# One transposition and one correction product per pair of tiles in a fused convolution, mixing and adapter kernel

## The chip, the cores and the metric

The kernel runs on 1 core of one Trainium2 chip. The metric is the device time of one execution in microseconds (us), and less is better. PE is the matrix engine, DVE the vector engine, ACT the scalar engine, POOL the general engine, SP the engine that here only issues transfers. "Ln" is line n of the kernel before.

## The reference

The input x has 128 samples of 64 channels by 1024 steps. Four residual layers follow each other. Layer 0 is a long convolution by channel, masked by length; layer 1 mixes the channels with one of 16 matrices; layers 2 and 3 are dense over the 1024 steps with low-rank adapters, chosen by one id of 32 (rank 16) and one label of 5 (rank 32).

```python
def _L2_cond_ref(x, adapter_ids, base_weight, base_bias, lora_A_w, lora_B_w):
    result = jnp.einsum('bsd,od->bso', x, base_weight) + base_bias
    A = lora_A_w[adapter_ids]
    Bw = lora_B_w[adapter_ids]
    h = jnp.einsum('bsd,brd->bsr', x, A)
    lora_out = jnp.einsum('bsr,bor->bso', h, Bw)
    return result + lora_out

def _L3_cond_ref(x, labeler_index, W, lora_A, lora_B_w):
    base = jnp.einsum('bsi,oi->bso', x, W)
    labelers_A = lora_A[labeler_index]
    low = jnp.einsum('bsi,bir->bsr', x, labelers_A)
    delta = jnp.einsum('bsr,or->bso', low, lora_B_w) * LORA_SCALING
    return base + delta

x = x + _L0_cond_ref(x, itok_B_8_3872, ...)
x = x + _L1_cond_ref(x, itok_B_0_15, ...)
x = x + _L2_cond_ref(x, itok_B_6_15, ...)
x = x + _L3_cond_ref(x, itok_B_0_2, ...)
```

## The kernel before

The work has three stages. In the **setup** (to about 177 us) PE multiplies the two dense layers, each with the identity added for the residual, into one 1024 by 1024 matrix. It also makes what the adapters need: `b2_0` to `b2_3` (the B factors of layer 2 carried through layer 3), `c` (how the layer-2 B factors meet the layer-3 A factors), the bias carried through layer 3 as one row (`row`, from `b3t`), and the bias against the layer-3 A factors (`c_row`). The setup is a list of jobs, `ORDER`; each has one of four areas of PSUM (the accumulators) and waits until the area's last user is read out. In the **convolution** (to about 545 us) PE runs one channel after the other. The **dense stage** (to the end) is the one that the change is about.

The dense stage takes the 128 samples as 64 tiles of two samples (128 rows: 2 by 64 channels), and two tiles (`v` = 0 and 1) make a pair `n`, so there are 32 pairs. Every engine has one written-out order per pair (`pair(n, last_one)` in `dense_tensor`, `dense_vector`, `dense_scalar`, `dense_sync`, `dense_gpsimd`) and runs it in order. Pairs 1 to 30 (to 29 on SP) are a hardware loop. Engines meet only at semaphores, and a wait holds everything behind it on its engine.

The two tiles are cut into halves `a11`, `a21`, `a22`, `a12` and multiplied with seven products in place of eight, after Strassen: M1, M5, M2, M4 (`wide_product`, L782: 24 instructions each, whose right half also carries 96 adapter columns) and M6, M3, M7 (`plain_product`, L792: 12 instructions each). Values are split into a high and a low part, in three passes. M1 and M2 share the accumulator S, M5 and M4 V, M6 and M7 P, M3 uses Q.

For the adapters of tile `v` the order is: DVE copies the low-rank values h out of PSUM to `hrow` (`h_rows`, L677); PE transposes them (`turn`, L772); DVE copies them to `hc` (`h_columns`, L685); PE multiplies with `c_gath` (`adapters`, L777), which adds to the layer-3 values what the layer-2 adapter and the bias put into them; DVE splits the result into `hs` (`h_stack`, L689); PE multiplies `hs` with the gathered B factors `stack` (`low_rank`, L800), once for the left and once for the right half of the outputs. `low_rank(0, 0)` ends by raising `lr11_done`. SP loads the rows of `stack` (`load_stack`, L434) and of `c_gath` (`load_c`, L475), after it has read ids into registers (`ids`, L409).

While PE works on pair `n`, it also mixes the channels for pair `n + 1` in four pieces, `quarter(n + 1, 0)` to `quarter(n + 1, 3)` (L759). All four write the same accumulator bank, `MIX_BANK`. ACT reads each piece out (`take`, L564) and raises `quarter_read`; the next piece waits for it:

```python
            if bank == MIX_BANK:
                ready(pe, quarter_read, 4 * n + q)
```

ACT's order in the middle of a pair stands at L598 to L609:

```python
            if not last_one:
                take(n + 1, 0, a11, xa11)
            act.wait_ge(lr11_done, n + 1)
            act.wait_ge(pair_sums, 2 * n + 2)
            copy(halves(y_out[0][:, 0:HB]), of_s, ACT.Copy).then_inc(y11_copied, 1)
            ...
            if not last_one:
                take(n + 1, 1, a21)
                h_high(act, n + 1, 0)
                h_high(act, n + 1, 1)
```

`h_high` (L442, its activations are L449) writes the high parts of the adapters' A factors of pair `n + 1` into the weights, and `h_low` (L458, L465) on DVE the low parts. After `h_low` DVE makes sums of the mixed pieces (`sums`, L669: L671, L672, L675), and then adds M7 to the output (L745), which raises `u3_read`; PE's last piece of a pair, `low_rank(1, HB)`, waits for it.

Of the kernel before, what the change touches and what calls it, by code (L numbers as in the profile page):

```python
# [12 lines left out]
P = 128  # L13
# [10 lines left out]
KC = 2 * R2 + 2  # L24
# [17 lines left out]
def program(nc, x, xt_in, steps, cond, adapter, labeler, log_dt, ssm_c, log_a_real, a_imag, ssm_d,  # L42
# [64 lines left out]
    ones, o = at("ones", [P, 1], F32, o)  # L107
# [27 lines left out]
    c_row, o = at("c_row", [1, LR], F32, o)  # L135
    assert o <= o_w[2]
# [82 lines left out]
    hc = both("hc", [P, P])  # L219
    hs = both("hs", [P, 2, P], F32R)  # L220
    c_gath = both("c_gath", [P, P])
    late = place("late", [P, HB], U16)
    assert o == o_last
    o += 8 * T
# [5 lines left out]
    hrow = both("hrow", [P, P])  # L230
# [10 lines left out]
    c_d = nc.dram_tensor("c_d", [AR + 1, LR], F32).ap()  # L241
    b3_d = nc.dram_tensor("b3_d", [R3, 2, T], F32).ap()
    row_d = nc.dram_tensor("row_d", [2, T], F32).ap()
# [51 lines left out]
    split_const, const_stored, b3_scaled = sem("split_const"), sem("const_stored"), sem("b3_scaled")  # L295
    bias_ready = sem("bias_ready")
# [66 lines left out]
    c_adapters = c_d[0:AR].rearrange("(a r) c -> a r c", r=R2)  # L363
# [49 lines left out]

    def load_tables(eng, v, a, l):
# [17 lines left out]
    masked = sem("masked")  # L432

    def load_stack(eng, v, a):  # L434

        for b in range(2):
            row = b * (R2 + R3)
            eng.dma_start(f(stack[v][row:row + R2]), b2_d[bass.ds(a[b], 1)].squeeze(0)).then_inc(stack_landed[v], 16)
            eng.dma_start(f(stack[v][KS + row:KS + row + R2, 0]),
                          b2_d[bass.ds(a[b], 1), :, 0, :].squeeze(0)).then_inc(stack_landed[v], 16)  # L440
# [27 lines left out]
    def dense_sync(sp):  # L468
# [6 lines left out]
        def load_c(v, a, l):  # L475
            for b in range(2):
                rows = slice(b * (R2 + R3), b * (R2 + R3) + R2)
                cols = bass.ds(l[b] * R3, R3)
                sp.dma_start(c_gath[v][rows, H3], c_adapters[bass.ds(a[b], 1), :, cols].squeeze(0)).then_inc(c_landed[v], 16)
                sp.dma_start(c_gath[v][KS + b:KS + b + 1, H3], c_d[AR:AR + 1, cols]).then_inc(c_landed[v], 16)  # L480
# [3 lines left out]
        for v in range(2):  # L484
            for to, of in ((stack[v][H3], b3_d), (stack[v][KS + R2:KS + R2 + R3, 0], b3_d[:, 0]), (stack[v][KS:KS + 2, 1], row_d)):
# [5 lines left out]
        sp.wait_ge(c_fixed, 2)  # L491
# [5 lines left out]
        def stacks(n):  # L497

            if isinstance(n, int) and n == 0:
                for v in range(2):  # L500
                    load_stack(sp, v, first_ids[v])
                return
            sp.wait_ge(p_done, n)
            for v in range(2):
                load_stack(sp, v, ids(sp, n, v, B))

        def pair(n, last_one):
# [7 lines left out]
            a, l = [ids(sp, n + 1, v, B) for v in range(2)], [ids(sp, n + 1, v, 2 * B) for v in range(2)]  # L515
# [3 lines left out]
            sp.wait_ge(adapted, 2 * n + 2)  # L519
# [9 lines left out]
    def dense_gpsimd(pool):  # L529
        pool.wait_ge(x1_stored[1], stored_all)  # L530
        for v in range(2):
            pool.wait_ge(x1_landed[v], LANDED_FIRST)
        for v in range(2):
            nc.gpsimd.tensor_copy(c_gath[v][:], ident[:]).then_inc(gfixed, 1)
        pool.wait_ge(gfixed, 4)
        for v in range(2):
            nc.gpsimd.memset(c_gath[v][:, KS:P], 0.0).then_inc(c_fixed, 1)
        pool.wait_ge(c_fixed, 2)
        fixed = [0]

        def fix(ins):
            fixed[0] += 1
            ins.then_inc(small_fixed, 1)
            pool.wait_ge(small_fixed, fixed[0])

        for v in range(2):
            fix(nc.gpsimd.memset(hrow[v][:], 0.0))
            fix(nc.gpsimd.memset(hc[v][:], 0.0))
# [1228 lines left out]
```

## Time and profile before

| | us |
|---|---|
| median of 3 runs | 1446.25 |
| lowest and highest run | 1444.93, 1446.51 |
| the profiled execution, its own time | 1442.18 |
| its span, first to last instruction | 1440.4 |
| PE busy in it | 1429.8 (99%) |
| DVE busy | 1127.4 (78%) |
| ACT busy | 612.7 (43%) |
| POOL busy | 100.9 (7%) |

The times of instructions are from the one profiled execution, counted from the start of its span. A matrix instruction's start is when it enters the engine, and the next one enters before it ends, so what a group costs PE is the distance between starts. When its result can be read is told by its end.

### The profile page before, as it was taken

The page shows a single profiled execution, that of the slowest core. Times are in us where ns is not written, and L with a number is a line of the kernel's source. Part 1 is how long each engine was busy: PE and PEld are TensorE (multiplying, and loading weights), DVE is VectorE, ACT ScalarE, POOL GpSimd, SP SyncE. Part 2 cuts the span into 40 slices and gives each one's busy share as a digit, 9 for nine tenths or more (in the row PEclk, how much of TensorE's full clock was granted, in tenths as well). Part 3 has the DMA queues.
Part 4 walks back from the last instruction along what each step waited for, and adds up shares of the span by engine and source line. Part 5 has one row for each costly group of instructions (what it writes and reads, how often), then busy time and mean ns, then how long its engine had stood idle before and what let it go on. Part 6 is the DMA issues. An engine that isn't in the chain of part 4 may idle for free.

```text
span 1440.4 us, 31629 instructions
## 1 busy us (share of the span) xinstructions
PE 1429.8 (99%) x9368; PEld 1329.8 (92%) x9368; DVE 1127.4 (78%) x2288; ACT 612.7 (43%) x1217; POOL 100.9 (7%) x193
## 2 busy tenths in 40 slices
PE   9999999999999999999999999999999999999998
PEld 7888899999999999999999999999999999999997
DVE  7975498888888887777777777787777777778775
ACT  4331376666666663333433433433343343343331
POOL 2322100000000002000000000000000000000000
PEclk9999999999999999999999999999999999999999
DMA  8033288888888886564564565556556556555652
GB/s 315 1 129 79 76 283 272 276 277 272 277 268 276 273 274 183 170 203 148 166 200 146 162 197 163 153 182 190 153 162 204 146 161 203 153 153 190 182 154 81
DMA packets 117070, 271.94 MB, mean 189 GB/s; under 512 B 24173, under 2 KB 60401, under 8 KB 114381
## 3 DMA queue, kind: packets, MB, share of 16 engines
q1 hardware_dynamic: 107048, 237.86, 54.1%
q10 hardware_dynamic: 9990, 33.68, 5.8%
q8 instruction: 17, 0.28, 0.1%
q14 instruction: 15, 0.12, 0.0%
HBM read 198.59 MB, written 72.85 MB: 188 GB/s over the span
## 4 chain that ended last, share of the span: by engine, by line
PE 95%; DVE 2%; DMA 2%; SPq 0%; issue 0%; POOL 0%; ACT 0%; DVEq 0%; POOLq 0%; ACTq 0%
PE ps L796 18%; PE ps L789 17%; PE ps L1704 14%; PE ps L788 12%; PE ps L769 8%; PE ps L1603 7%; PE ps L1715 6%; PE ps L805 4%; PE ps L1695 3%; PE ps L1707 2%; PE ps L1589 1%; PE ps L780 1%; PE ps L1612 1%; DMA p<-in_L_cond_base_weight 1%; DMA out<-y_out 1%; PE ps L775 1%
## 5 line engine op out<-in xcount | busy, mean ns | idle before, releaser
L789 PE MATMUL ps<-weights,xa 128*128 128x352 f32 x1152 | 323.0, 322 | 0.0
L788 PE MATMUL ps<-weights,xa 128*128 128x256 f32 x1152 | 321.8, 281 | 0.5 <-ACT y_out L597 0.5
L796 PE MATMUL ps<-weights,xs 128*128 128x512 f32 x1152 | 291.2, 401 | 0.0
L796 PEld LDWEIGHTS ps<-weights,xs 128*128 128x128 f32 x1152 | 207.0, 189 | 40.4
L1704 PE MATMUL ps<-toep,ut 128*128 128x512 f32 (+2 forms) x1152 | 226.7, 342 | 0.0
L788 PEld LDWEIGHTS ps<-weights,xa 128*128 128x128 f32 x1152 | 217.3, 189 | 2.5 <-issue 1.1
L789 PEld LDWEIGHTS ps<-weights,xa 128*128 128x128 f32 x1152 | 216.2, 188 | 1.3
L1704 PEld LDWEIGHTS ps<-toep,ut 128*128 128x128 f32 x1152 | 194.3, 189 | 16.6
L568 ACT ACTIVATE a<-ps 128x512 f32<-128x512 f32 x128 | 76.7, 599 | 281.9 <-PE ps L769 281.2
L769 PE MATMUL ps<-m_gath,x_in 128*128 128x128 f32 x1024 | 134.6, 275 | 1.3 <-DVE x_in L660 1.3
L769 PEld LDWEIGHTS ps<-m_gath,x_in 128*128 128x128 f32 x1024 | 126.6, 191 | 4.0 <-DVE x_in L660 1.5
L1196 ACT ACTIVATE ut<-xt 128x896 fp32r<-128x896 f32 x64 | 61.2, 956 | 138.4 <-PE ps L1715 131.0
L651 DVE COPY_PREDICATED x_in<-late,x_nat 128x512 f32<-128x512 uint16 x124 | 92.8, 748 | 18.9 <-DVE late L646 18.7
L1715 PE MATMUL ps<-toep,ut 128*128 128x256 f32 x768 | 107.3, 289 | 0.0
L789 PE MATMUL ps<-weights,xs 128*128 128x352 f32 x384 | 106.6, 320 | 0.0
L788 PE MATMUL ps<-weights,xs 128*128 128x256 f32 x384 | 105.2, 278 | 0.0
L382 POOL COPY m_gath<-mix 64x64 f32 x128 | 49.5, 387 | 788.8 <-PE ps L769 689.2
L1603 PE MATMUL ps<-p,staged 128*128 128x512 f32 x432 | 99.1, 390 | 0.0
L1603 PEld LDWEIGHTS ps<-p,staged 128*128 128x128 f32 x432 | 80.8, 188 | 18.0 <-DVE c_row L1474 0.9
L1715 PEld LDWEIGHTS ps<-toep,ut 128*128 128x128 f32 x768 | 95.8, 190 | 0.0
L1523 DVE TENSOR_TENSOR ut<-xt,ut 128x896 fp32r<-128x896 f32 x64 | 69.9, 1092 | 16.2 <-ACT ut L1196 16.2
L449 ACT ACTIVATE weights<-tab 128x128 fp32r<-128x128 f32 (+1 forms) x256 | 71.5, 354 | 23.1 <-DVE tab L456 23.1
(227 smaller groups left out, 2255.3 us busy)
## 6 DMA issues: line engine op xcount, KB each, us to landing
xt<-in_xt SPq DMA_DIRECT2D x64, 512.0 KB, 5.7
x_d<-yo SPq DMA_DIRECT2D x64, 512.0 KB, 2.9
x_nat<-in_x SPq DMA_DIRECT2D x64, 512.0 KB, 3.8
lags<-kern_d SPq DMA_DIRECT2D x63, 512.0 KB, 5.0
x_in<-x_d SPq DMA_DIRECT2D x62, 512.0 KB
out<-y_out ACTq DMA_DIRECT2D x62, 512.0 KB, 5.8
stack<-b_d SPq DMA_DIRECT2D x130, 128.0 KB, 3.9
tab<-a_d SPq DMA_DIRECT2D x128, 128.0 KB, 2.1
```

The source lines that it names most:

```text
L449: ins = nc.scalar.activation(to, of, ACT.Copy)
L568: ins = copy(raw[:], mixing, ACT.Copy)
L651: nc.vector.copy_predicated(x1_in[v][:, cols], late[:], x_nat[v][:, cols]).then_inc(chosen[v], 1)
L769: ins = mm(acc[:, bank, i * P:(i + 1) * P], x1_in[v][:, c * P:(c + 1) * P], m_gath[v][:], start=True, stop=True)
L788: mm(acc[:, left, 0:HALF], x_part, w[:, 0:HALF], start=start, stop=end, skip_group_check=True)
L789: ins = mm(acc[:, right, 0:HALF + KR], x_part, w[:, HALF:WIDE], start=start, stop=end, skip_group_check=True)
L796: ins = mm(acc[:, bank], operand[:, a, i, :], plain(i, b, m), start=opens and i == a == b == 0, stop=i == K4 - 1 and a == 1, skip_group_ch ...
L1196: copy(ut[u % 2][:, 0, 0:SPLIT], xt[u % BUFS][:, 0:SPLIT], ACT.Copy).then_inc(ut_hi, 1)
L1523: tt(ut[u % 2][:, 1, 0:SPLIT], xt[u % BUFS][:, 0:SPLIT], f(ut[u % 2][:, 0, 0:SPLIT]), ALU.subtract).then_inc(ut_lo, 1)
L1603: ins = mm(t[:, cols], staged[n % 2][:, a, c, :], p3[:, c, b, cols], start=c == a == b == 0, stop=c == K8 - 1 and a == 1)
L1704: mm(y[:, half * HB + i * P:(half + 1) * HB], xs[:, a, half * half_t + i, :], tp[:, b, 0:HB - i * P], start=i == a == b == 0, stop=False)
L1715: ins = mm(y[:, to:to + QT], xs[:, a, i, :], tp[:, b, at_col:at_col + QT], start=False, stop=i == half_t - 1 and a == 1)
```

## The change

The dense stage now handles both tiles of a pair together in `turn` and `adapters`:

- `hrow`, `hc` and `c_gath` exist once, with tile 0 in rows or columns 0 to 63 and tile 1 in 64 to 127. `turn(n)` transposes both tiles at once, between the halves of M6; the one inside M4 is gone. `adapters(n)` is one product, after `quarter(n + 1, 1)`.
- `low_rank(0, 0)` and its `lr11_done` come behind M3 instead of behind M6, directly ahead of `quarter(n + 1, 2)`.
- On DVE one `h_columns(n)` comes after `first_low(n + 1)`, and both `h_stack` come after the addition of M6 (L738).
- The bias no longer passes through `c_gath`. The setup makes one bias row per label (`row_d` has 5 rows of two parts), for which `c_row` is made earlier, behind the job `a3b`, turned by five small products into `crt`, and multiplied with `b3n`. The job `row` so has four products of 512 columns (each two instructions) in place of two, and waits for `b3_scaled` and `crt_ready`. SP loads the chosen labels' rows into `stack` in every pair: 12 transfers of `stack` and 4 of `c_gath` per pair, before 8 and 8.
- Tile 1 has its high and low parts in the other order of rows, so that DVE reads and writes its 64 rows where they lie.
- SP reads four ids with one load (`pair_ids`).
- ACT's order in the dense stage is as it was.

```diff
+    HIGH, LOW = (0, KS), (KS, 0)
+    def load_stack(eng, v, a, l):
...
+            high, low, bias = HIGH[v] + row, LOW[v] + row, LOW[v] + 2 * b
+            eng.dma_start(f(stack[v][high:high + R2]), b2_d[bass.ds(a[b], 1)].squeeze(0)).then_inc(stack_landed[v], 16)
+            eng.dma_start(f(stack[v][low:low + R2, 0]), b2_d[bass.ds(a[b], 1), :, 0, :].squeeze(0)).then_inc(stack_landed[v], 16)
+            eng.dma_start(f(stack[v][bias:bias + 2, 1]), row_d[bass.ds(l[b], 1)].squeeze(0)).then_inc(stack_landed[v], 16)
...
             h_rows(n, 0)
-            h_columns(n, 0)
             if not last_one:
                 choose(n + 1, 1, 0)
             dve.wait_ge(m4_done, n + 1)
             h_rows(n, 1)
-            h_stack(n, 0)
-            h_columns(n, 1)
             if not last_one:
                 first_low(n + 1)
+            h_columns(n)
+            if not last_one:
                 choose(n + 1, 1, 1)
-            h_stack(n, 1)
             dve.wait_ge(m6_done, n + 1)
             dve.wait_ge(pair_sums, 2 * n + 2)
             tt(y_out[0][:, HB:T], y_out[1][:, HB:T], of_p, ALU.add).then_inc(u2_read, 1)
+            for v in range(2):
+                h_stack(n, v)
...
-            wide_product(xa22, M4, V_LEFT, V_RIGHT, FRONT, False)
-            turn(n, 0)
-            wide_product(xa22, M4, V_LEFT, V_RIGHT, BACK, False).then_inc(m4_done, 1)
-            adapters(n, 0)
+            wide_product(xa22, M4, V_LEFT, V_RIGHT, ALL, False).then_inc(m4_done, 1)
             if not last_one:
                 quarter(n + 1, 0)
             pe.wait_ge(s2_lo, n + 1)
             ready(pe, y22_added, n)
             plain_product(xs2, M6, P_BANK, FRONT, True)
-            turn(n, 1)
+            turn(n)
             plain_product(xs2, M6, P_BANK, BACK, False).then_inc(m6_done, 1)
-            pe.wait_ge(hs_lo, 2 * n + 1)
-            pe.wait_ge(stack_landed[0], 64 * n + 64)
-            if isinstance(n, int) and n == 0:
-                pe.wait_ge(rows_landed, 16 * 6)
-            low_rank(0, 0, PIECES_S).then_inc(lr11_done, 1)
-            adapters(n, 1)
             if not last_one:
                 quarter(n + 1, 1)
+            adapters(n)
             pe.wait_ge(s4_lo, n + 1)
             ready(pe, y12_added, n)
             plain_product(xs4, M3, Q_BANK, ALL, True)
+            pe.wait_ge(hs_lo, 2 * n + 1)
+            pe.wait_ge(stack_landed[0], 96 * n + 96)
+            if isinstance(n, int) and n == 0:
+                pe.wait_ge(rows_landed, 16 * 4)
+                pe.wait_ge(stack_cleared, 1)
+            low_rank(0, 0, PIECES_S).then_inc(lr11_done, 1)
             if not last_one:
                 quarter(n + 1, 2)
...
-            over_chunks(t[0:1, HB + LR:HB + 2 * LR], lambda c: bias_col[:, c:c + 1], lambda c: a3raw[:, c, :]).then_inc(job_done, 1)
+            for l in range(L3N):
+                ins = mm(t[0:R3, HB + LR + l:HB + LR + l + 1], c_row[:, l * R3:(l + 1) * R3], ones[0:1, 0:1], start=True, stop=True)
+            ins.then_inc(job_done, 1)
             t = job("row")
             pe.wait_ge(bias_ready, 1)
+            pe.wait_ge(b3_scaled, 1)
             for half in range(2):
                 cols = slice(half * HB, (half + 1) * HB)
-                ins = mm(t[0:1, cols], ones[:], b3t[:, cols], start=True, stop=True)
+                mm(t[0:L3N, cols], ones[:], b3t[:, cols], start=True, stop=False)
+            pe.wait_ge(crt_ready, 1)
+            for half in range(2):
+                cols = slice(half * HB, (half + 1) * HB)
+                ins = mm(t[0:L3N, cols], crt[B3_ROWS], b3n[B3_ROWS, cols], start=False, stop=True)
```

How the instructions move is shown for the loop over the pairs. First PE before, from M6 to M7 (`xs2` to `xs3`; `m_gath` with `x1_in` is a quarter, `stack0` with `hs0` is `low_rank(0, ...)`):

```order
L796 MATMUL ps<-weights_49,xs2_158 128x512 x6
L805 MATMUL ps<-stack0_171,hs0_178 128x256 [waits stack_landed0,hs_lo]
L805 MATMUL ps<-stack0_171,hs0_178 128x256 x3
L780 MATMUL ps<-hc1_177,c_gath1_181 128x128 [waits hc_ready,c_landed1]
...
L769 MATMUL ps<-m_gath1_187,x1_in1_175 128x128 [waits quarter_read]
L769 MATMUL ps<-m_gath1_187,x1_in1_175 128x128 x3
L796 MATMUL ps<-weights_49,xs4_159 128x512 [waits y12_added,x_s4_lo]
L796 MATMUL ps<-weights_49,xs4_159 128x512 x11
...
L769 MATMUL ps<-m_gath1_187,x1_in1_175 128x128 [waits quarter_read]
```

The same stretch of PE in the change:

```order
L804 MATMUL ps<-weights_49,xs2_160 128x512 x6
...
L775 MATMUL ps<-m_gath1_187,x1_in1_177 128x128 [waits quarter_read]
L775 MATMUL ps<-m_gath1_187,x1_in1_177 128x128 x3
...
L788 MATMUL ps<-hc_178,c_gath_181 128x128 [waits hc_ready,hs_lo,c_landed1,c_landed0]
L804 MATMUL ps<-weights_49,xs4_161 128x512 [waits y12_added,x_s4_lo]
L804 MATMUL ps<-weights_49,xs4_161 128x512 x11
...
L813 MATMUL ps<-stack0_173,hs0_179 128x256 [waits stack_landed0]
L813 MATMUL ps<-stack0_173,hs0_179 128x256 x3
...
L775 MATMUL ps<-m_gath1_187,x1_in1_177 128x128 [waits quarter_read]
```

The first `low_rank` stood ahead of the second quarter; now it stands behind M3, directly ahead of the third quarter (the last row of both pieces). The correction product (`hc` with `c_gath`) has moved behind the second quarter.

ACT in the change, from its reading of the first quarter to that of the third; the same instructions stood in the same order before:

```order
L572 ACTIVATE a11_166<-ps 128x512 [waits mixed]
L574 ACTIVATE xa11_156<-ps 128x512
L605 ISA [waits lr11_done]
L606 ACTIVATE y_out0_171<-ps 128x512 [waits pair_sums]
...
L572 ACTIVATE a21_167<-ps 128x512 [waits mixed]
...
L461 ACTIVATE weights_49<-tab2_0_190 128x4x2x16 [waits tab_landed0]
...
L461 ACTIVATE weights_49<-tab2_1_184 128x4x2x16 [waits diffed]
...
L572 ACTIVATE a22_168<-ps 128x512 [waits mixed]
```

Nothing moved on ACT: its wait for `lr11_done` stands ahead of its reading of the second quarter (`a21`) in both.

## Rows read from the trace of the kernel before

**Rows 1.** The page: PE's busy time, and the granted clock in 40 slices
```profile
PE 1429.8 (99%) x9368; PEld 1329.8 (92%) x9368; DVE 1127.4 (78%) x2288; ACT 612.7 (43%) x1217; POOL 100.9 (7%) x193
...
PEclk9999999999999999999999999999999999999999
```

**Rows 2.** Waits of PE, whole span: us in total, times, longest
```profile
PE ps L769 <- DVE x_in L660: 1.3, 1, 1.3
PE ps L788 <- ACT y_out L597: 0.5, 1, 0.5
```

**Rows 3.** Timeline of PE, 814 to 831 us: start, length, engine, line, what, count
```profile
816.25 0.38 PE L780 MATMUL ps<-hc,c_gath 128*128 128x128 f32 x2
816.46 1.06 PE L769 MATMUL ps<-m_gath,x_in 128*128 128x128 f32 x8
817.28 1.63 PE L796 MATMUL ps<-weights,xs 128*128 128x512 f32 x6
...
820.24 0.64 PE L805 MATMUL ps<-stack,hs 128*128 128x256 f32 x4
820.72 0.39 PE L780 MATMUL ps<-hc,c_gath 128*128 128x128 f32 x2
820.95 1.06 PE L769 MATMUL ps<-m_gath,x_in 128*128 128x128 f32 x8
821.76 3.00 PE L796 MATMUL ps<-weights,xs 128*128 128x512 f32 x12
824.60 1.05 PE L769 MATMUL ps<-m_gath,x_in 128*128 128x128 f32 x8
...
829.97 0.72 PE L805 MATMUL ps<-stack,hs 128*128 128x512 f32 x2
830.52 0.29 PE L788 MATMUL ps<-weights,xa 128*128 128x256 f32 x1
830.64 0.32 PE L789 MATMUL ps<-weights,xa 128*128 128x352 f32 x1
```

**Rows 4.** Timeline of ACT, same pair
```profile
821.00 0.60 ACT L602 ACTIVATE y_out<-ps 128x512 f32<-128x512 f32 x1 [2.36 <-PE ps L805]
822.04 0.60 ACT L568 ACTIVATE a<-ps 128x512 f32<-128x512 f32 x1 [0.44 <-PE ps L769]
822.53 1.11 ACT L449 ACTIVATE weights<-tab 128x128 fp32r<-128x128 f32 x4
```

**Rows 5.** Timeline of DVE, same pair
```profile
816.44 0.42 DVE L682 COPY hrow<-ps 64x48 f32<-64x48 f32 x2
...
819.26 0.67 DVE L667 TENSOR_TENSOR xa<-a,xa 128x512 fp32r<-128x512 f32 x1
...
821.14 0.42 DVE L692 CAST hs<-ps 64x256 fp32r<-64x256 f32 x1
...
826.80 0.69 DVE L671 TENSOR_TENSOR s<-a,a 128x512 f32<-128x512 f32 x1 [0.42 <-ACT xa L570]
...
828.80 0.68 DVE L745 TENSOR_TENSOR y_out<-y_out,ps 128x512 f32<-128x512 f32 x1
```

**Rows 6.** Timeline near 591 us, the dense stage's one wait of PE
```profile
590.61 0.60 ACT L597 ACTIVATE y_out<-ps 128x512 f32<-128x512 f32 x1 [2.99 <-DMA out<-y_out]
...
591.36 0.36 PE L788 MATMUL ps<-weights,xa 128*128 128x256 f32 x1 [0.52 <-ACT y_out L597]
...
591.55 0.32 PE L789 MATMUL ps<-weights,xa 128*128 128x352 f32 x1
```

**Rows 7.** Timeline at 1403 us, a pair whose adapter tables had landed early
```profile
1402.95 2.13 ACT L449 ACTIVATE weights<-tab 128x128 fp32r<-128x128 f32 x8
...
1404.10 2.24 DVE L465 TENSOR_TENSOR weights<-tab,weights 128x128 fp32r<-128x128 f32 x8 [0.54 <-ACT weights L449]
```

**Rows 8.** Timeline of the setup, PE and DVE
```profile
105.24 1.88 PE L1670 MATMUL ps<-b3t,ones 128*1 128x512 f32 x4
...
129.03 4.24 PE L1679 MATMUL ps<-fac_v,fac_u 128*32 128x32 f32 x128
...
104.03 1.23 DVE L1416 TENSOR_TENSOR b_out<-ps,b_out 128x1024 fp32r<-128x1024 f32 x1 [4.96 <-ACT b_out L1134]
...
110.09 0.68 DVE L1478 TENSOR_SCALAR b3t<-b3t 32x1024 f32<-32x1024 f32 x1 [1.73 <-DMA b3t<-in_L_cond_lora_B_w]
```

More of the change, by code:

```diff
@@ L23 @@
 KS = 2 * R2 + R3
-KC = 2 * R2 + 2
 ROUND = 1.5 * 2.0 ** 23
@@ L135, in program @@
     c_row, o = at("c_row", [1, LR], F32, o)
+    b3n, _ = at("b3n", [P, T], F32, o_c - AR // P * 4 * T)
     assert o <= o_w[2]
@@ L229, in program @@
     m_gath = both("m_gath", [P, P])
-    hrow = both("hrow", [P, P])
+    hrow = place("hrow", [P, P])
     x_nat[1], o = at("x_nat1", [P, T], F32, o_rest + 4 * T + 4 * TFOLD)
@@ L476, in load_c @@
             for b in range(2):
[L477 to L480, printed above, removed]
+                row = v * KS + b * (R2 + R3)
+                to = c_gath[row:row + R2, v * KS + R2:v * KS + R2 + R3]
+                sp.dma_start(to, c_adapters[bass.ds(a[b], 1), :, bass.ds(l[b] * R3, R3)].squeeze(0)).then_inc(c_landed[v], 16)
         sp.dma_start(x1_d[:, C - 1], yo[(C - 1) % 2][:]).then_inc(x1_stored[1], 16)
@@ L484, in dense_sync @@
         for v in range(2):
-            for to, of in ((stack[v][H3], b3_d), (stack[v][KS + R2:KS + R2 + R3, 0], b3_d[:, 0]), (stack[v][KS:KS + 2, 1], row_d)):
+            high, low = HIGH[v] + R2, LOW[v] + R2
+            for to, of in ((stack[v][high:high + R3], b3_d), (stack[v][low:low + R3, 0], b3_d[:, 0])):
                 sp.dma_start(f(to), of).then_inc(rows_landed, 16)
@@ L514, in pair @@
             stacks(n)
-            a, l = [ids(sp, n + 1, v, B) for v in range(2)], [ids(sp, n + 1, v, 2 * B) for v in range(2)]
+            a, l = pair_ids(n + 1, B), pair_ids(n + 1, 2 * B)
             for v in range(2):
@@ L770, in quarter, with turn, adapters @@
             ins.then_inc(mixed, 1)
-        def turn(n, v):
-            pe.wait_ge(hrow_ready, 2 * n + v + 1)
-            ready(pe, hs_lo, 2 * n + v)
-            nc.tensor.transpose(acc[:, SMALL_BANK, 0:P], hrow[v][:], ident[:]).then_inc(turned, 1)
-        def adapters(n, v):
-            pe.wait_ge(c_landed[v], 64 * n + 64)
-            pe.wait_ge(hc_ready, 2 * n + v + 1)
-            mm(acc[:, SMALL_BANK, P:2 * P], c_gath[v][:], hc[v][:], start=True, stop=True).then_inc(adapted, 1)
+        def turn(n):
+            pe.wait_ge(hrow_ready, 2 * n + 2)
+            ready(pe, hc_ready, n)
+            nc.tensor.transpose(acc[:, SMALL_BANK, 0:P], hrow[:], ident[:]).then_inc(turned, 1)
+        def adapters(n):
+            for v in range(2):
+                pe.wait_ge(c_landed[v], 32 * n + 32)
+            pe.wait_ge(hc_ready, n + 1)
+            ready(pe, hs_lo, 2 * n)
+            mm(acc[:, SMALL_BANK, P:2 * P], c_gath[:], hc[:], start=True, stop=True).then_inc(adapted, 1)
         def wide_product(operand, m, left, right, chunks, opens):
@@ L800, in low_rank @@
         def low_rank(v, col, pieces):
-            for j, rows in ((0, P), (1, KS + 2)):
+            for j, rows in ((0, P), (1, (KS + 4, P)[v])):
                 at_col = col
@@ L894, in _ @@
             sp.dma_start(a3_d.rearrange("l p n -> p l n"), lora3_out[:].rearrange("p l c r -> p l (c r)")).then_inc(a3_stored, 16)
+            sp.dma_start(b3n[B3_ROWS], lora3_b).then_inc(in_b3, 16)
             for m in range(4):
```

131 lines of the change are left out of this document (66 added, 65 removed).

## The prediction, on record before the changed kernel ran

> **What bounds the kernel now.** I read the engines' busy times first: PE is busy for 1429.8 of 1440.4 us at the full granted clock, and no other engine is near it [rows 1]. Then PE's waits: in the 32 pairs of the dense stage it waits once, for 0.5 us [rows 2]. So what PE no longer does is a gain, and any new wait of PE is a loss, one for one. Last I read the timelines of one pair, since the change moves work past waits, and a busy total can't tell how late each of them is [rows 3 to 5].
>
> **What PE saves.** One transposition: M6 with one inside takes 2.96 us from start to start (817.28 to 820.24), M3 with the same 12 products takes 2.84 (821.76 to 824.60) [rows 3]. That is 0.12 us, and I take it for the one inside M4. One correction product: 0.21 us (816.25 to 816.46) or 0.23 (820.72 to 820.95) [rows 3], so 0.22. Together 0.34 us per pair, 10.9 us in 32 pairs.
> The Trainium skill ("TensorE: Matmul & The Clock Gate", Part 4: PE-mode transpose) gives a 128 by 128 transposition about 275 ns in one kernel's context. By that 32 of them would save 8.8 us and not 3.8, and the sum would come out 5 us lower. The row has the transposition overlapped by its neighbours, so I keep 0.12.
>
> **What is moved without cost.** Count from the end of M4, 816.25. DVE has `hrow` copied at +0.6 [rows 5]; `turn` now comes at +2.3 (a quarter of 0.82, half of M6). Its result is there near +2.6; DVE is then in `first_low`, which was over at +3.7 [rows 5] and now starts 0.2 earlier, so `hc` is ready near +3.8. `adapters` comes at 0.82 + 2.96 + 0.81 = +4.6: 0.8 us to spare. DVE then has two mask steps and one copy under mask (about 1.3 us), the addition of M6 (0.7) and the two `h_stack` (L692 with 0.42 [rows 5] and a subtraction, about 0.7 each). The first is ready near +6, and `low_rank(0, 0)` comes at 4.6 + 0.22 + 2.84 = +7.7. Nothing waits there. On SP, 12 plus 4 transfers stand for 8 plus 8, and four loads of ids for twelve, so the adapter tables come no later by more than the 2 us of four `stack` issues; the chain below reads them over 2 us later than today. POOL's preparation is about as long as it was. I cost these at nothing; if SP came much later, `h_high` would wait and everything below grow with it.
>
> **The new wait, first part.** `low_rank(0, 0)` raises `lr11_done`. ACT stands at that wait before it reads the second quarter, and the third quarter may not start until that reading is done, since they share a bank. Before, the product came ahead of the second quarter, and ACT had its copy L602 behind it while PE did the second quarter and M3. Now the product is the last thing ahead of the third quarter. Let S be its start. ACT's copy starts at S + 0.76 (820.24 to 821.00 [rows 3, 4]). The reading L568 can follow 0.49 later (the distance of ACT's next two starts, 822.04 to 822.53) and takes 0.60 [rows 4]: done at S + 1.85. PE restarts 0.15 after such an end (591.21 to 591.36 [rows 6]): S + 2.00. Without the wait it would be S + 0.48 (820.24 to 820.72 [rows 3]). So PE stands for 1.52 us. The pipe's refill costs 0.07: the product after the restart is 0.19 behind (591.36 to 591.55), else 0.12 (830.52 to 830.64) [rows 6, 3].
>
> **Second part.** Behind that reading ACT writes the adapters' high parts for both tiles, now 3.6 us later against M6 than before. They start at S + 1.25 + 0.49 = S + 1.74. DVE's low parts start 1.15 behind and take 2.24 where nothing else holds them [rows 7]: S + 5.13. Then come the sums and L745, whose start is 2.00 behind the first sum's (826.80 to 828.80) and which takes 0.68 [rows 5]: S + 7.81, and with 0.15 PE may start its last piece, which waits for `u3_read`, at S + 7.96. PE itself is there at S + 2.07 + 5.37 = S + 7.44 (third quarter to last piece, 824.60 to 829.97 [rows 3]). So it waits 0.52 and refills for 0.07.
>
> **The setup.** The job `row` gets two more products, 4 instructions of 0.47 each: 1.88 us; 10 instructions of one column at the price of the smallest shown, 4.24 / 128 = 0.033 each: 0.33 us [rows 8]. It also waits for `b3_scaled`. DVE ends the last `b2` part at 105.26, then scales for 0.68 [rows 8]; a copy of one row moved ahead of it adds some 0.3: 106.2, with 0.15 for the restart 106.4. PE is there at 105.24 + 0.33 = 105.6. So 0.8 of wait, 3.0 us in all, all of it on PE's path. Bounds: 2.2 without that wait, 4 if the transfer of `b3n` or the small products are later.
>
> **The sum.** Per pair 1.52 + 0.07 + 0.52 + 0.07 - 0.34 = +1.84 us. The waits exist only where a next pair is mixed, in 31 pairs: +57.0. The last pair saves 0.34. With the setup: 57.0 - 0.3 + 3.0 = +59.7 us. Against the profiled execution's own 1442.18 that gives 1501.9. That execution lies 4.1 us below the median of the runs, 1446.25; the same difference on the median gives **1506 us**.
>
> **Rivals.**
> (a) Only the first wait is there: DVE or ACT run a little tighter than the rows laid end to end, and the last piece finds `u3_read` up. For it: 0.52 us is a small difference of two long chains. Against it: each distance in the chain is one that the trace shows without a wait in it. Then 1.52 + 0.07 - 0.34 = 1.25 per pair, +38.8 - 0.3 + 3.0: 1488.
> (b) A third wait. M2 and M4 wait for ACT's copies L592 and L597, which wait for the stores of the pair before; PE has already lost 0.5 us there once [rows 2, 6]. The output is finished later against the next M1 than today, and more `stack` transfers start sooner beside the stores. At that row's price, 0.5 us in each of 31 pairs, +15.5: 1522.
> (c) It gets faster. The third quarter's wait costs nothing, because the reading of the second quarter is over by then. That holds if ACT reads the quarter ahead of its wait for `lr11_done`, or if that product comes 1.5 us or more ahead of the third quarter. Then only the saving and the setup are left: -10.9 + 3.0, 1438. The order on ACT and PE in the change speaks against both: the product stands directly ahead of the quarter, and ACT's wait ahead of the reading.
> (d) The waits let the granted clock fall. PE has waited 1.3 us ahead of the dense stage with no slice below full [rows 1, 2], and the new waits are 1.5 us and shorter, with longer stretches of products between them. I give it no case of its own.
>
> **How the numbers follow.** The forecast with both waits has 0.72, (a) 0.12, (b) 0.12, (c) 0.03, and 0.01 is left for no change. The range from 1486 to 1524 takes in (a) and (b) with the bounds of the setup. Within 0.2% (3 us), which is about what a measurement of this kernel can tell from no change, I give 0.01; faster 0.03; slower 0.96.
>
> **What would show it.** PE's waits should have a row for L775 (the quarters) behind ACT's reading L572, 31 times, about 1.5 us each, and one for L813 (`low_rank`) behind DVE L751, 31 times, about 0.5 us. PE's busy time should fall by about 8 us (10.9 saved, 2.2 added) while the span grows by 60. ACT's wait for PE ahead of L606 should grow, since the product comes 3 us later against M6. A distance from pair to pair that has not grown, or waits of PE behind SP's transfers or behind L596 and L601, would make the prediction wrong. If the change is slower but these two rows are not there, the reason is wrong too.

## The result, and the profile after

| | before | changed |
|---|---|---|
| median of 6 runs | 1445.29 us (1443.25 to 1446.51) | 1534.06 us (1530.36 to 1538.81) |
| span of the profiled execution | 1440.4 us | 1532.1 us |
| ratio, 95% interval | | 1.0617 [1.0595, 1.0638] |

The change makes the kernel 6.2% slower. I had forecast slower, and 1506 us; the time lies 28 us above that and outside my range of 1486 to 1524.

The page of the changed kernel, the lines that answer to [rows 1]:

```profile
PE 1451.6 (95%) x9286; PEld 1327.1 (87%) x9286; DVE 1118.6 (73%) x2256; ACT 601.7 (39%) x1217; POOL 96.4 (6%) x187
...
PEclk9999999999999999999999999999999999999999
```

The granted clock is full in every slice (mean 1.000), so the loss is not TensorE's clock: PE stands. Its waits, and two of ACT's (us in total, times, longest), which answer to [rows 2]:

```profile
ACT y_out L606 <- PE ps L813: 205.7, 32, 12.5
...
ACT y_out L596 <- DMA out<-y_out: 97.1, 30, 4.2
...
PE ps L775 <- ACT a L572: 39.0, 31, 1.3
...
PE ps L796 <- ACT y_out L596: 22.5, 29, 1.8
...
PE ps L813 <- DVE y_out L751: 8.2, 31, 0.3
...
PE ps L1682 <- DVE b3n L1479: 2.3, 1, 2.3
```

The two waits that I had forecast are there, 31 times each. The row between them is one that I had only as a rival: PE's M2 (L796) waits for ACT's copy L596 of M1's result, and that copy waits for a store.

One pair of the changed kernel, the timeline of all engines cut to the chain (start, length, engine, line, what, count):

```profile
880.56 0.39 PE L788 MATMUL ps<-hc,c_gath 128*128 128x128 f32 x2
...
880.70 3.02 PE L804 MATMUL ps<-weights,xs 128*128 128x512 f32 x12
...
883.56 0.63 PE L813 MATMUL ps<-stack,hs 128*128 128x256 f32 x4
884.31 0.60 ACT L606 ACTIVATE y_out<-ps 128x512 f32<-128x512 f32 x1 [6.23 <-PE ps L813]
884.80 0.59 ACT L572 ACTIVATE a<-ps 128x512 f32<-128x512 f32 x1
885.28 2.13 ACT L461 ACTIVATE weights<-tab 128x128 fp32r<-128x128 f32 x8
...
885.45 1.16 PE L775 MATMUL ps<-m_gath,x_in 128*128 128x128 f32 x8 [1.26 <-ACT a L572]
...
886.36 2.98 PE L804 MATMUL ps<-weights,xs 128*128 128x512 f32 x12
886.43 2.24 DVE L477 TENSOR_TENSOR weights<-tab,weights 128x128 fp32r<-128x128 f32 x8 [3.26 <-ACT weights L461]
...
890.12 1.05 PE L775 MATMUL ps<-m_gath,x_in 128*128 128x128 f32 x8
890.70 0.69 DVE L751 TENSOR_TENSOR y_out<-y_out,ps 128x512 f32<-128x512 f32 x1
...
891.36 0.86 SPq L482 DMA_DIRECT2D x_in<-x_d  x2
...
891.44 0.74 PE L813 MATMUL ps<-stack,hs 128*128 128x512 f32 x2 [0.27 <-DVE y_out L751]
...
892.01 0.35 PE L796 MATMUL ps<-weights,xa 128*128 128x256 f32 x1
...
892.14 0.34 ACTq L623 DMA_DIRECT2D out<-y_out  x1
...
898.84 0.60 ACT L596 ACTIVATE y_out<-ps 128x512 f32<-128x512 f32 x1 [3.18 <-DMA out<-y_out]
...
899.58 0.36 PE L796 MATMUL ps<-weights,xa 128*128 128x256 f32 x1 [0.62 <-ACT y_out L596]
```

Read it from S = 883.56, the start of the moved product. ACT copies at S + 0.75, reads the second quarter until S + 1.83, and PE goes on at S + 1.89; I had S + 2.00. DVE's L751 starts at S + 7.14 and PE's last piece at S + 7.88; I had S + 7.96. Then comes the wait that my sum had at nothing. SP issues the two loads of x1 at 891.36, since they wait only for the last quarter. The store, on ACT's queue, waits for DVE's sums, which are late, and goes out at 892.14, 0.78 us behind the first load. It lands when ACT's copy starts, at 898.84. In the kernel before, the first load went out 0.03 us ahead of the store, and the second 0.50 us behind it.

Where a pair's time went, from first product to first product in the trace, where nothing else is said (means over the 32 pairs, in the last two columns over the 31 that have a next one; us). M1, M5, M2 and M4 follow each other in this order, and a product here is two instructions, of which the first counts:

| | M1 to M5 | M5 to M2 | M2 to M4 | M4, first to last product | M4's last to the next M1 | pair |
|---|---|---|---|---|---|---|
| before | 3.30 | 3.29 | 3.34 | 3.20 | 14.56 | 27.68 |
| changed | 3.39 | 4.18 | 3.44 | 3.08 | 16.39 | 30.52 |

The pairs take 31 x 2.84 = 88.1 us more, the setup 4.9. The last pair, from its M1 to the end of the span, takes 1.3 less (28.16 for 29.46). The span grew by 91.7.

### The profile page after: what moved, and what is told of

Read it like the earlier page. It is cut to its first block, busy times and chain, and to the rows that moved or that the text cites. A ratio compares the mean times of both kernels' runs of the same rounds, so it can differ in the third digit from the quotient of the medians.

```text
span 1532.1 us, 31101 instructions
## 1 busy us (share of the span) xinstructions
PE 1451.6 (95%) x9286; PEld 1327.1 (87%) x9286; DVE 1118.6 (73%) x2256; ACT 601.7 (39%) x1217; POOL 96.4 (6%) x187
## 4 chain that ended last, share of the span: by engine, by line
PE 73%; DMA 14%; DVE 4%; issue 4%; ACT 4%; SPq 0%; POOL 0%; ACTq 0%; DVEq 0%; POOLq 0%
PE ps L804 17%; PE ps L1720 13%; DMA out<-y_out 13%; PE ps L797 9%; PE ps L775 8%; PE ps L796 7%; PE ps L1731 6%; PE ps L1610 4%; PE ps L1711 3%; PE ps L813 3%; PE ps L1723 2%; ACT a L572 1%; ACT y_out L596 1%; PE ps L1619 1%; ACT xa L574 1%
## 5 line engine op out<-in xcount | busy, mean ns | idle before, releaser
L796 PE MATMUL ps<-weights,xa 128*128 128x256 f32 x1152 | 326.1, 284 | 22.7 <-ACT y_out L596 22.5
L796 PEld LDWEIGHTS ps<-weights,xa 128*128 128x128 f32 x1152 | 217.2, 189 | 36.5 <-issue 36.3
L477 DVE TENSOR_TENSOR weights<-tab,weights 128x128 fp32r<-128x128 f32 (+1 forms) x256 | 71.8, 354 | 101.0 <-ACT weights L461 101.0
L796 PE MATMUL ps<-weights,xs 128*128 128x256 f32 x384 | 106.3, 280 | 0.0
L606 ACT ACTIVATE y_out<-ps 128x512 f32<-128x512 f32 x32 | 19.1, 597 | 205.7 <-PE ps L813 205.7
```

The lines of the kernel that those rows point to most:

```text
L477: ins = nc.vector.tensor_tensor(to, of, f(high), ALU.subtract)
L796: mm(acc[:, left, 0:HALF], x_part, w[:, 0:HALF], start=start, stop=end, skip_group_check=True)
```

## The experiments

Ratios are to the kernel before, run in turn with each kernel on the same chip. "Head start" is the time from the issue of the first x1 load to that of the first tile's store; "landing" is the time from the store's issue to the start of ACT's copy that waits for it. Both are medians over 26 pairs.

**1. ACT's order exchanged** (changed kernel; e1_act_order)

```diff
+            if not last_one:
+                take(n + 1, 1, a21)
+                h_high(act, n + 1, 0)
+                h_high(act, n + 1, 1)
             act.wait_ge(lr11_done, n + 1)
...
             if not last_one:
-                take(n + 1, 1, a21)
-                h_high(act, n + 1, 0)
-                h_high(act, n + 1, 1)
                 act.wait_ge(a22_lo, n + 1)
```

> The change, with ACT reading the second quarter and writing both tiles' high parts ahead of its wait for lr11_done. Theory (the order on ACT behind that wait makes PE's waits at the third quarter and at the last low_rank): both rows of PE, 39.0 and 8.2 us of waiting in the change, go to 0. The third wait (M2 behind ACT's copy of M1, 22.5 us) follows from the order in which transfers start: if it comes from the stack transfers starting sooner against the store, it falls below 8 us, since without the two waits the store starts 0.2 us sooner against M1 and the stack transfers 0.5 us later; the time is then 1436 to 1446 us. Rival A (the third wait has its own cause in the change, whatever the two others do): it stays above 18 us and the time is about 1465. Rival B (the two waits come from the single correction product or from DVE's order, not from ACT's): the rows stay, 1520 or more.

Measured: 1437.57 us (1437.02 to 1438.77), ratio 0.9947 [0.9931, 0.9964]. PE's waits:

```profile
PE ps L1683 <- DVE b3n L1480: 2.4, 1, 2.4
...
PE ps L797 <- ACT y_out L596: 0.8, 1, 0.8
...
PE ps L814 <- DVE y_out L752: 0.4, 1, 0.4
```

Of the three rows of the pairs the first has gone, and the two others are left with one time each. A pair takes 27.32 us against 27.64 (medians): 0.32 saved, and I had forecast 0.34. So everything that the change loses in the pairs comes from ACT's order against the moved product. With it put right, the change is a gain.

**2. Only the reading of the second quarter ahead of the wait; the adapters' high parts stay behind it**

```diff
+            if not last_one:
+                take(n + 1, 1, a21)
             act.wait_ge(lr11_done, n + 1)
...
-                take(n + 1, 1, a21)
                 h_high(act, n + 1, 0)
```

> The change, with only the reading of the second quarter ahead of ACT's wait for lr11_done; the high parts stay behind it. Theory (two chains from the same product): the wait at the third quarter goes (39.0 us to 0), but PE's wait at the last low_rank behind DVE grows from 8.2 us to about 45 (1.5 us in each of 31 pairs), since that chain gets only 0.5 us shorter while PE comes 1.4 us sooner. Per pair 0.5 us less, so 1515 to 1522 us. Rival (the second wait is only an after-effect of the first): it stays at 8 us or less and the time falls by 45 us, to 1490 or less.

Measured: 1491.42 us (1486.86 to 1493.48), ratio 1.0326 [1.0309, 1.0343]. PE's longest row of waits:

```profile
PE ps L814 <- DVE y_out L752: 39.4, 31, 1.3
```

The first wait went, and the second grew from 0.3 to 1.3 us: PE comes 1.4 us earlier (it goes on at S + 0.47 and not at S + 1.89) to a point that DVE's chain sets, and that point moved by only 0.5 (S + 7.40 for S + 7.88). That part held. The time is still 24 us below what I expected, because the third wait went as well: the head start of the x1 loads was now 1.78 us, and the store landed in 4.62 us. So a late store alone doesn't make the third wait: it goes out 0.13 us after M1's start here as in the changed kernel. This was the first sign that the head start counts.

**3. The kernel before with one part of the change: the first `low_rank` behind M3**

```diff
-            pe.wait_ge(hs_lo, 2 * n + 1)
-            pe.wait_ge(stack_landed[0], 64 * n + 64)
...
-            low_rank(0, 0, PIECES_S).then_inc(lr11_done, 1)
...
             plain_product(xs4, M3, Q_BANK, ALL, True)
+            pe.wait_ge(hs_lo, 2 * n + 1)
+            pe.wait_ge(stack_landed[0], 64 * n + 64)
...
+            low_rank(0, 0, PIECES_S).then_inc(lr11_done, 1)
```

> The kernel before, with one edit: low_rank(0, 0), which raises lr11_done, stands behind M3 instead of behind M6. Two transpositions, two correction products, the bias in c_gath, single id loads and the setup are as before. Theory (that place alone makes the loss): waits of PE at the third quarter of about 1.3 us in 31 pairs and at the last low_rank appear, and the time is 1500 to 1535 us, by whether the store is late as well. If the third wait needs SP's faster id loads, it stays below 8 us here and the time is 1500 to 1512. Rival (the loss comes from handling both tiles together): below 1465.

Measured: 1555.98 us (1554.41 to 1556.89), ratio 1.0764 [1.0746, 1.0782].

```profile
PE ps L769 <- ACT a L568: 38.9, 31, 1.3
PE ps L788 <- ACT y_out L592: 33.8, 30, 3.2
...
PE ps L775 <- DVE hrow L682: 0.7, 4, 0.2
```

The move alone brings the waits. The second one is in no row here, since each idle time, 0.13 us, is too short for that list; it shows in the distance from the fourth quarter to the last piece, 1.18 us for 0.81. The time lies 21 us above the range that I had expected and 22 above the changed kernel's. A pair takes 31.37 us, 0.85 more than in the changed kernel. 0.32 of that is what the change saves in a pair. M4 takes 0.2 us longer than in the kernel before (3.41 for 3.20), and the last row, PE ahead of the transposition inside M4, stands for it: `hrow` is late. The third wait is larger, 1.1 us each for 0.8 (M5 to M2 takes 4.50 us): the store lands 7.1 us after its issue on the mean, and 6.8 in the changed kernel. Why it lands later stays open.

**4. Is it the stack transfers?** (changed kernel; SP holds them back until ACT has copied M1)

```diff
-            sp.wait_ge(p_done, n)
+            sp.wait_ge(m1_copied, n + 1)
```

> The change, with SP starting a pair's stack transfers only when ACT has begun to copy M1 (it waits for m1_copied in place of p_done), so that none is under way while the store of the pair before is landing. Theory (the stack transfers, sooner and more of them, hold up the store that M2 waits for): PE's wait of M2 behind ACT's copy of M1 falls from 22.5 us to under 6, the store lands within 5.5 us of its issue, and the time is 1504 to 1512. Rival (the two x1 loads, which now start 0.8 us ahead of the store and not with it, hold it up): the wait stays at 18 to 26 us and the time at 1530 to 1536.

Measured: 1540.25 us (1539.59 to 1541.82), ratio 1.0661 [1.0644, 1.0679].

```profile
PE ps L775 <- ACT a L572: 39.0, 31, 1.3
PE ps L796 <- ACT y_out L596: 24.3, 30, 1.7
PE ps L813 <- DVE y_out L751: 8.2, 31, 0.3
```

The stack transfers now started 7.7 us after M1's start, behind the store's landing, and the row stayed. My prediction had named them as one of the two reasons for rival (b); they are not the cause. The store landed 6.77 us after its issue, with a head start of 0.78 us as in the changed kernel. The time is 6 us above the changed kernel's and 4 above the range for this rival; 4 of the 6 are in the pairs (30.65 us each for 30.52).

**5. The x1 loads held back beside the store** (changed kernel)

```diff
+            if not isinstance(n, int) or n > 0:
+                sp.wait_ge(p_done, n)
             for v in range(2):
                 load_x1(n + 1, v)
```

> The changed kernel, but SP issues the two x1 loads of the pair after next only when PE's last piece of the pair is done, so that they go out beside the store of the pair's output and no longer 0.6 to 0.8 us ahead of it. Theory (order of arrival: a store that is issued behind the loads waits for their megabyte, one that is issued with them gets in between): the store lands within 5.2 us in place of 6.8, the row of PE's M2 waiting for ACT's copy L596 (22.5 us) goes, the two other rows stay at 39 and 8 us, and the time falls by 22 to 25 us to 1508 to 1513 us. Rival (the store is late for the whole of the traffic or for the time at which it is issued): the row stays within 5 us of 22.5 and the time stays at 1530 to 1538.

Measured: 1502.27 us (1500.93 to 1504.08), ratio 1.0385 [1.0368, 1.0402]. One pair's timeline:

```profile
884.29 0.34 ACTq L625 DMA_DIRECT2D out<-y_out  x1
...
884.57 0.86 SPq L482 DMA_DIRECT2D x_in<-x_d  x2
...
887.17 0.64 ACT L595 ACTIVATE xs<-s 128x512 fp32r<-128x512 f32 x1 [0.29 <-DVE s L715]
...
887.81 0.60 ACT L598 ACTIVATE y_out<-ps 128x512 f32<-128x512 f32 x1
```

The loads went out 0.27 us behind the store. ACT's copy L598 waited for nothing, so the store was there at most 3.5 us after its issue. The row of M2 is gone, and the two others are as they were (39.0 and 8.1 us). The time fell by 31.8 us, more than the 22 to 25 that I had expected: M5 to M2 is back at 3.29 us and M2 to M4 at 3.35, which is 0.89 + 0.09 = 0.98 us per pair, or 30 us. I had reckoned with the row's total alone, and a row of waits tells less than the wait costs (see the last section).

**6. Only the second x1 load held back** (changed kernel)

```diff
-            for v in range(2):
-                load_x1(n + 1, v)
+            load_x1(n + 1, 0)
+            if not isinstance(n, int) or n > 0:
+                sp.wait_ge(p_done, n)
+            load_x1(n + 1, 1)
```

> As the run before, but only the second of the two x1 loads waits for PE's last piece; the first keeps its head start. Theory (order of arrival, 512 KB at a time): one load ahead of the store costs half of what two cost or, where it is nearly through, nothing: landing 5.2 to 6.0 us, the row of M2 behind L596 at 0 to 10 us, 1508 to 1522 us. Rival (any head start of a load delays the store fully): landing 6.8 us, row 22 us, 1530 to 1538 us.

Measured: 1516.6 us (1508.82 to 1520.11), ratio 1.0502 [1.0484, 1.0519]; landing 5.78 us, M2's row 4.2 us in 8 times. The profile is of the fastest run, 1508.82, so in the others the row may be larger. The result lies in between, as the order of arrival has it: one load of 512 KB ahead of the store costs part of what two cost.

**7. The fault put into the good version**: experiment 1, with the store held back until PE is through the first two products (four instructions) of the next M1, where it raises `m1_begun`

```diff
                 act.wait_ge(y11_copied, n + 1)
+                act.wait_ge(m1_begun, n + 2)
                 act.dma_start(out_rows[bass.ds(2 * n, 1)].squeeze(0), y_out[0][:]).then_inc(y_stored[0], 16)
...
+                    if mark is not None and i == 0 and (a, b) == PASSES[1]:
+                        ins.then_inc(mark, 1)
...
-            wide_product(xa11, M1, S_LEFT, S_RIGHT, ALL, True).then_inc(m1_done, 1)
+            wide_product(xa11, M1, S_LEFT, S_RIGHT, ALL, True, m1_begun).then_inc(m1_done, 1)
```

> The kernel of e1_act_order (1437.6 us, no wait of PE in the pairs), but the store of the pair's first tile waits for PE's second pair of products of the next M1, so that it is issued 0.6 to 0.8 us behind the x1 loads in place of 0.04. Nothing else is moved. Theory (order of arrival): the store lands 6.7 us after its issue in place of 5.2, at 7.4 us after M1's start; ACT's copy and with it M2 come late by 1.3 us in each of 30 pairs, and the time is 1437.6 + 31 x 1.4 = 1481 us (1465 to 1490). Rival (the order plays no part and the store takes 5.2 us from its issue): landing at 5.9, copy done at 6.5, where PE needs it at 6.5: 1437 to 1442 us.

Measured: 1477.64 us (1474.35 to 1482.6), ratio 1.021 [1.019, 1.023]. PE's waits, then one pair:

```profile
PE ps L799 <- ACT y_out L597: 36.5, 30, 2.6
```

```profile
906.10 0.86 SPq L483 DMA_DIRECT2D x_in<-x_d  x2
...
907.17 0.34 ACTq L626 DMA_DIRECT2D out<-y_out  x1
...
913.34 0.60 ACT L597 ACTIVATE y_out<-ps 128x512 f32<-128x512 f32 x1 [3.68 <-DMA out<-y_out]
...
914.08 0.36 PE L799 MATMUL ps<-weights,xa 128*128 128x256 f32 x1 [1.13 <-ACT y_out L597]
```

A store issued 1.04 us later landed 2.01 us later (7.13 us against 5.12 after M1's start). So one half of the 2.01 is the later issue itself, and the other half, 0.97, is a longer way with the same loads further ahead. By the rival it would have landed at 6.16, ACT's copy of 0.60 us would have been done at 6.76, and PE, which needs it at 6.6, would have stood for about 0.3 us a pair with the restart. It stands for 1.2, and M5 to M2 takes 4.57 us for 3.28. So most of the third wait comes from the head start, in a kernel that has neither of the other two; the lateness of the store adds the rest. The head start was 1.08 us and not the 0.6 to 0.8 that I had aimed at, and the landing 6.2 us, not 6.7.

**8. The setup's order on DVE** (experiment 1, with one step earlier)

```diff
+            dve.wait_ge(in_b3, 16)
+            ts(b3n[B3_ROWS], b3n[B3_ROWS], 0.5, None, ALU.mult).then_inc(b3_scaled, 1)
             b2_low(2, b2_out)
             b2_low(3, b2_out)
-
-            dve.wait_ge(in_b3, 16)
-            ts(b3n[B3_ROWS], b3n[B3_ROWS], 0.5, None, ALU.mult).then_inc(b3_scaled, 1)
```

> The kernel of e1_act_order, but DVE scales b3n ahead of the third part of b2 and no longer behind the fourth, where it took 2.62 us from start to end while POOL's L1038 ran, for 0.68 in the kernel before with POOL idle. Theory (the scaling stood behind POOL's instruction on the way to SBUF): there it takes 0.7 to 1.3 us, PE's wait of 2.4 us for b3n ahead of the job row goes, and the time is 1434.5 to 1436 us. Rival (the wait of PE ahead of the job row is then for crt, or the setup's end is set by another chain): 1437 to 1438 us.

Measured: 1434.90 us (1433.56 to 1437.66), ratio 0.9919 [0.9903, 0.9936]. The changed kernel's setup, all engines:

```profile
105.29 2.34 POOL L1038 TENSOR_TENSOR staged<-p,staged 128x1024 fp32r<-128x1024 f32 x1 [3.82 <-ACT staged L1111]
...
105.54 0.47 PE L1675 MATMUL ps<-ones,c_row 1*32 1x1 f32 x10
...
105.55 2.62 DVE L1479 TENSOR_SCALAR b3n<-b3n 32x1024 f32<-32x1024 f32 x1
...
108.32 1.88 PE L1682 MATMUL ps<-b3t,ones 128*5 128x512 f32 x4 [2.31 <-DVE b3n L1479]
...
110.13 1.88 PE L1686 MATMUL ps<-b3n,crt 32*5 32x512 f32 x4
...
111.94 1.43 PE L1610 MATMUL ps<-p,staged 128*128 128x512 f32 x5
```

and the same steps with the scaling moved:

```profile
97.20 0.68 DVE L1477 TENSOR_SCALAR b3n<-b3n 32x1024 f32<-32x1024 f32 x1
...
106.24 0.47 PE L1676 MATMUL ps<-ones,c_row 1*32 1x1 f32 x10
...
106.64 1.88 PE L1683 MATMUL ps<-b3t,ones 128*5 128x512 f32 x4
```

The scaling takes 0.68 us where POOL is idle. Beside POOL's L1038 it ends 0.54 us after POOL's instruction, as if it had hardly begun before. PE's wait of 2.3 us is gone; by the medians the kernel is 2.7 us faster than experiment 1, though the intervals of the two ratios still touch. The row of PE is the proof, not the time.

**9. Another cure: the moved product between the halves of M3** (changed kernel)

```diff
-            plain_product(xs4, M3, Q_BANK, ALL, True)
+            plain_product(xs4, M3, Q_BANK, FRONT, True)
...
             low_rank(0, 0, PIECES_S).then_inc(lr11_done, 1)
+            plain_product(xs4, M3, Q_BANK, BACK, False)
```

> The changed kernel with ACT's order as it is there, but the first low_rank stands between the halves of M3 and no longer behind it: 1.42 us further ahead of the third quarter. Theory (what costs is only how closely that product stands ahead of the quarter, and the other two waits are its consequences): the quarter's wait falls from 1.26 to 0 to 0.2 us, the wait behind DVE L751 and the one behind ACT's copy L596 (the x1 loads no longer go ahead of the store) both go, and the time is 1438 to 1450 us. Rival (hs is not ready 2.9 us after M6, so that PE waits for it in the middle of M3 instead, or the third wait stays by itself): 1455 us or more, with a row for L813 behind DVE's h_stack, or one of 22 us for L796 behind L596.

Measured: 1493.60 us (1490.86 to 1496.65), ratio 1.0333 [1.0317, 1.0349], 44 us above the top of what I expected.

```profile
PE ps L796 <- ACT y_out L596: 27.2, 30, 2.8
PE ps L813 <- DVE y_out L751: 7.8, 31, 0.3
```

The first wait is gone, the others stay. My theory was too simple: the second wait doesn't follow from the first. ACT still writes the high parts behind its copy of the product, so DVE's L751 starts 7.15 us after the product (902.03 to 909.18 in one pair), 7.14 in the changed kernel. PE has the half M3 more to do on the way, but no longer stands 1.4 us, so it arrives at the last piece as early as before. And as long as that piece is set by DVE's sums, the store is too, while the x1 loads are not: head start 0.76 us, landing 6.79, third wait. So it is the second wait that brings the third, not the first. It does so only while the head start is about as long as here: in experiment 2, with the second wait at its longest and a head start of 1.78, the third was gone.

**10. The version of experiment 8 once more, with more rounds**

> The fastest version so far once more with more rounds: the changed kernel with both of ACT's orders exchanged in the pairs and b3n scaled ahead of the third part of b2. Expected 1433 to 1437 us, ratio to the kernel before 0.991 to 0.994; by the rows 10.9 us are saved in the pairs and 2.2 to 3 us are left of the setup's cost.

Measured: 1434.75 us (1433.71 to 1436.22), ratio 0.9931 [0.9917, 0.9944]. It beats both kernels: 10 us below the one before, 99 below the changed one.

Head start and landing over all kernels (medians, us):

| kernel | head start | landing |
|---|---|---|
| 5 | -0.27 | at most 3.51 |
| before, 1, 8, 10 | 0.03 to 0.04 | 5.17 to 5.23 |
| 3 | 0.64 | 6.89 |
| 6 (one load only) | 0.75 | 5.78 |
| 9, changed, 4 | 0.76 to 0.78 | 6.74 to 6.79 |
| 7 | 1.08 | 6.16 |
| 2 | 1.78 | 4.62 |

SP issues the two loads about 0.53 us apart (0.96 in experiment 6). A store issued ahead of both is quick, one that comes between them takes 1.7 us more, and one that comes right behind both another 1.6. From there the landing gets shorter the more of the loads is through.

The transfers' own packets show where the store stands. In the changed kernel, for the 4.14 us after the store's issue (892.14 to 896.28), the trace has packets of SP's queue (q1) alone; then, to the landing, nearly all are ACT's (q10; the second tile's store is in them too). Columns are packets, MB, share of the 16 engines:

```profile
q1 hardware_dynamic: 237, 0.91, 89.7%
```

```profile
q10 hardware_dynamic: 235, 0.89, 85.0%
q1 hardware_dynamic: 52, 0.15, 15.8%
```

In the kernel before, the store's first packet comes 1.9 us after its issue, and from there to the landing (832.3 to 835.57) both queues move:

```profile
q1 hardware_dynamic: 190, 0.71, 62.6%
q10 hardware_dynamic: 144, 0.52, 39.2%
```

Over the pairs (medians of 30) the first packet of the store comes 0.84 us after its issue in experiment 5, 2.0 in the kernel before and 4.1 in the changed one, where 0.9 of the loads' 1.05 MB had started by then. So a store that is issued behind both loads starts only when they are nearly through.

The Trainium skill says ("DMA: Bandwidth & Descriptors", Queues, rings and completion order) that each DMA engine takes turns between the queues it has work for, a packet at a time. Where both queues move, in the kernel before, the packets fit that. But if the store's packets were ready from its issue, it would share with the loads from the first one on, and a head start could only help it. These runs show the contrary from 0.03 to 0.78 us; here the measurement decides. Why the packets start so late, whether they are made late or wait in their queue, no run shows.

## Why the prediction was right and wrong

- **What PE saves**: 0.34 us per pair forecast, 0.32 measured (experiment 1). M4 from first to last product went from 3.20 to 3.05 us there, so the transposition was worth 0.15, not 0.12; the correction product and what goes with it 14.56 - 14.39 = 0.17, not 0.22. The 275 ns that the Trainium skill gives for a transposition ("TensorE: Matmul & The Clock Gate", Part 4) would be nearly twice what it cost between other products.
- **What is moved without cost**: right. No row of PE's waits names `hs`, `hc`, `stack` or the tables in the changed kernel. Two distances in the text were too short, without an effect on the sum: the product comes 3.9 us later against M6, not 3, and the high parts 3.3 us (2.29 to 5.61), not 3.6. ACT's waits for the product grew with it, from 82.8 to 205.7 us in 32 times.
- **The first wait**: 1.52 + 0.07 forecast. Measured S to restart 1.89, without the wait 0.48: 1.41, and the quarter after it took 0.91 in place of 0.81: 0.10.
- **The second wait**: 0.52 + 0.07 forecast. The last piece starts 1.32 us after the fourth quarter's start (890.12 to 891.44), without a wait 0.81: 0.51; M1 then takes 3.39 for 3.31: 0.08. The two waits together cost 2.10 us for a forecast of 2.18. A chain laid end to end from distances that the trace shows without a wait in them was good to 0.1 us. Rival (a) is refuted by the row itself.
- **The step that failed** is the sum per pair, 1.52 + 0.07 + 0.52 + 0.07 - 0.34: it has two waits, and the third stood at 0 in it, as rival (b) with a chance of 0.12. The third is there in nearly every pair and costs 0.89 + 0.10 = 0.99 us, 31 us in all, which is more than the 28 us by which I was off. I had the place right (L796 behind L596 behind the store) and half the price: 0.5 us, from the one time it had occurred [rows 6]. Of my two reasons the `stack` transfers were wrong (experiment 4). That the output finishes later against the next M1 is true for 0.2 us (the store goes out 0.13 us after M1's start and no longer 0.08 ahead of it), of the 1.8 us by which ACT's copy comes later (6.87 us after M1's start for 5.10). The other 1.6 are the longer landing: I didn't ask what else is issued there. My own chain had the answer: it put the last sums 0.5 us behind PE, the store waits for the sums, the x1 loads for the quarter ahead of them. So the loads had to get about that far ahead (they got 0.77 us ahead, from 0.03).
- **Luck in the number**: on the span the forecast was short by 32 us (59.7 for 91.7), not 28. The other 4 came from the 4.1 us that I added between the profiled execution and the median: the changed kernel's profiled execution is its median run, so that addition had nothing to stand for. The 32 are the third wait (31) and the setup (1.9), less 1.0 that the last pair saved beyond my 0.3, and the rest cancels to 0.1.
- **The setup**: 3.0 forecast, 4.9 measured (107.05 to 111.94 for the first product of the next job). The products came out as reckoned: the four more at 1.81, the small ones at 0.47 for 0.33, and their start 0.3 later. The wait for `b3n` was 2.3 for 0.8, since DVE's scaling took 2.62 us beside POOL and not 0.68. The bound of 4 was too low too: I had taken the duration from a row in which POOL was idle. Experiment 8 shows the duration back at 0.68 and the wait gone.
- **The clock** (rival d): full throughout (mean 1.000), with PE's longest wait at 2.3 us.
- **Rival (c)**, faster if ACT reads the quarter ahead of its wait, 1438 us: experiment 1 is not quite that kernel (the high parts go ahead too), and gave 1437.6. Reading the quarter ahead alone gave 1491, and the product 1.4 us earlier gave 1494. So that rival's two conditions (the latter by 0.1 us not quite met) were both too weak: the second wait has to go as well.

## What to carry to other kernels

When an edit moves the point that signals another engine, look at everything that stands behind that engine's wait in its order; here one exchange of four lines on ACT turned a loss of 6% into a gain of 0.5% (0.7% with the setup's order). When a chain is delayed, ask of each DMA on both queues whether it waits for the delayed point or for one ahead of it: where a large load no longer has to wait for what its neighbour store waits for, their order turns round, and the store's reader pays. And a new wait found as a rival in the right place deserves its own sum over all pairs before it is given a small chance.

## What the runs showed of the hardware

- **A store's landing depends on which loads were issued just ahead of it on the other queue**: 512 KB landed within 3.5 us when it was issued first, in 5.2 between two loads of 512 KB, in 6.8 right behind both, in 4.6 with the loads 1.8 us ahead. Behind both, its first packet started 4.1 us after its issue, when 0.9 of 1.05 MB of the loads had started.
- **DVE can stand behind POOL**: 32x1024 f32 scaled from SBUF to SBUF took 2.62 us while POOL worked, 0.68 alone. Copies from PSUM in the kernel before (0.66 and 0.32 us, beside POOL's instruction at 105.02) were not held up. The Trainium skill's rule ("SBUF — State Buffer", Who interferes with whom), that DVE in its mode with two ports and POOL take a shared pair of ports for a whole instruction and the second one waits, fits all of these rows; which mode DVE was in no row shows.
- **A row of waits understates**: PE's three rows of the pairs add up to 69.7 us, but the pairs got 88.1 us longer although 10 were saved, so the waits cost 98. The difference is about 0.3 us for each of the 91 waits. It shows as PE's busy time, which I had expected to fall by 8 us and which rose by 21.8. By the trace, in which the ends of products are modelled, the product ahead of a wait is no longer overlapped by the next; and the ones after the restart come slower (the quarter takes 0.91 us for 0.81, M1 3.39 for 3.31).
